# Slot attention's last group: six complete token tiles' outputs are made inside the last levels of its scan

## What is computed

```python
q, k = short_conv(h @ Wq, cq), short_conv(h @ Wk, ck)
v, w = short_conv(h @ Wv, cv), l2norm(short_conv(h @ Ww, cv))
g, beta = log_sigmoid(h @ Wf1 @ Wf2), sigmoid(h @ Wb)
# scan over the tokens, 16 heads of 128 x 128 states Sk and Sv:
#   Sk = Sk * exp(g) + k (beta w)^T ;  Sv = Sv * exp(g) + (beta w) v^T
#   o = softmax(q Sk / sqrt(128)) Sv
gate = h @ Wg1 @ Wg2 + bg2
o = o * rsqrt(mean(o * o) + EPS)
o = o * norm_w * sigmoid(gate)
x = x + o @ Wo
```

## Time and profile before

| what | us |
|---|---|
| median of 3 runs (lowest, highest) | 2630.3 (2629.23, 2631.29) |
| the profiled execution's own time | 2630.27 |
| its span in the profile | 2628.5 |
| PE busy | 2331.3 (89%) |
| DVE, ACT, POOL busy | 1678.3, 1192.8, 1100.5 |

### The profile page before, as it was taken

How to read it: one execution, slowest core, us unless ns; L and a number is a source line. 1 busy time by engine, 2 the same in 40 slices (tenths; PEclk the granted TensorE clock), 3 DMA queues, 4 the chain that set the end, 5 groups by cost and what they waited for, 6 DMA issues and landing times. The chain is left out here.

```text
span 2628.5 us, 49074 instructions
## 1 busy us (share of the span) xinstructions
PE 2331.3 (89%) x18400; PEld 1614.6 (61%) x18400; DVE 1678.3 (64%) x3286; ACT 1192.8 (45%) x2937; POOL 1100.5 (42%) x1264
## 2 busy tenths in 40 slices
PE   5888888888888889888858999999889989999999
PEld 3467754777547775477745666677533356666685
DVE  3857777577776777667726777752366557777613
ACT  3655465554554546545424555532115535555411
POOL 0367632676326763277634544430030025444300
PEclk9999999999999999999978999999889989999999
DMA  2100000000010000000004000000100030000000
GB/s 46 49 6 2 2 17 32 6 2 2 17 33 5 3 2 17 17 2 2 2 1 120 19 19 19 7 1 1 49 1 1 1 114 19 19 19 13 1 1 17
DMA packets 57625, 46.30 MB, mean 18 GB/s; under 512 B 11560, under 2 KB 50864, under 8 KB 57008
## 3 DMA queue, kind: packets, MB, share of 16 engines
q1 hardware_dynamic: 57392, 43.16, 5.6%
HBM read 42.10 MB, written 1.05 MB: 16 GB/s over the span
## 5 line engine op out<-in xcount | busy, mean ns | idle before, releaser
L1153 DVE SCALAR_TENSOR_TENSOR work<-four,taps,work 128x511 f32<-128x511 f32 (+2 forms) x384 | 284.7, 748 | 127.1 <-ACT work L849 117.5
L1761 POOL TENSOR_TENSOR rot<-q_plain,ropes 128x512 f32<-128x512 f32 x64 | 81.0, 1266 | 574.7 <-ACT q_plain L1792 574.7
L599 PE MATMUL four<-xT,wring 128*128 128x512 f32 x512 | 252.8, 621 | 6.6 <-DMA wring<-in_Wk_dram 4.8
L906 ACT ACTIVATE work<-four 128x512 f32<-128x512 f32 x216 | 129.0, 597 | 269.4 <-PE four L678 243.4
L729 PE MATMUL four<-work 128*128 128x128 f32 x1536 | 217.0, 286 | 0.0
L1805 ACT ACTIVATE pr<-four,nmaxf 128x512 f32<-128x512 f32 (+3 forms) x256 | 133.8, 525 | 171.4 <-DVE nmaxf L1643 171.4
L1643 DVE TENSOR_REDUCE nmaxf<-four 128x1 f32<-128x512 f32 (+3 forms) x256 | 125.7, 491 | 125.6 <-PE four L1486 120.8
L729 PEld LDWEIGHTS four<-work 128*128 128x128 f32 x1536 | 193.4, 196 | 3.9
L1484 PE MATMUL four<-rot,rot 128*128 128x512 f32 (+3 forms) x512 | 179.5, 446 | 5.5 <-DVE rot L1635 3.8
L1088 POOL TENSOR_TENSOR work<-work 128x256 f32<-128x256 f32 x184 | 145.6, 791 | 78.0 <-DVE work L1217 57.4
L1095 POOL TENSOR_TENSOR work<-work 128x256 f32<-128x256 f32 x184 | 141.7, 770 | 84.2 <-PE bank L763 74.6
(11 more groups left out here) (266 smaller groups left out, 5430.9 us busy)
## 6 DMA issues: line engine op xcount, KB each, us to landing
wqkv<-in_f_wq_dram SPq DMA_DIRECT2D x32, 128.0 KB, 2.3
wqkv<-in_f_wk_dram SPq DMA_DIRECT2D x32, 128.0 KB, 2.4
wqkv<-in_f_wv_dram SPq DMA_DIRECT2D x32, 128.0 KB, 2.4
wo<-in_f_wo_dram SPq DMA_DIRECT2D x2, 2048.0 KB, 11.7
we<-in_f_we_dram SPq DMA_DIRECT2D x4, 1024.0 KB
wring<-in_Wk_dram SPq DMA_DIRECT2D x4, 512.0 KB, 3.8
wring<-in_Ww_dram SPq DMA_DIRECT2D x4, 512.0 KB
wring<-in_Wv_dram SPq DMA_DIRECT2D x4, 512.0 KB, 3.9
```

The source lines that it names most:

```text
L599: last = nc.tensor.matmul(unit_bank(i)[:], wring[n % 2][:, c, h * P:(h + 1) * P], k.xT[:, c, b * T:(b + 1) * T], start=(c == 0), stop=(c = ...
L906: nc.scalar.activation(turned_keys(s, l), b3(key_bank), ACT.Copy).then_inc(key_kept, 1)
L1153: ins = nc.vector.scalar_tensor_tensor(out=cbuf[i % 4][:, n:], in0=unit_bank(i)[:, 0:T - n], scalar=taps[:, {"q": 0, "k": 1}.get(kind, 2), ...
```

## The change

The tiles of the last group are taken in a new order, 0, 1, 2, 4, 5, 6 and then 3 and 7 (`LAST_TILES`, `tile_of`). Eight steps are woven into the scan's end: `LATE` gives e = 0 to 5 to (s, j) = (8, 1) to (8, 6), e = 6 to (9, 0) and e = 7 to (9, 1). In step e, at the end of the level's own work:

- PE makes gate(e), then turn_y(e - 1) for e = 1 to 6, then result(e - 2) for e = 2 to 7;
- ACT does open_gate(e) and keep_y(e - 1);
- DVE does bias(e), scale_y(e - 1), add(e - 2);
- POOL scales tile e (for e up to 5), and at (8, 0), after its decay (6,4), takes the root of the six complete tiles (24 elements per partition).

Behind the scan POOL takes the root of the other two tiles (8 elements) and scales them, and turn_y, keep_y, result and add follow for these two. All eight gates are made in the scan. The last group's gate, y and yT buffers lie in work areas that are free by then, and its three products use PSUM banks 0, 2 and 3. The first of each waits for the last use of its bank.

```diff
+LATE = {(B * CH, j): j - 1 for j in range(1, LEVELS)} | {(B * CH + 1, 0): LEVELS - 1, (B * CH + 1, 1): LEVELS}
+LAST_TILES = [b * CH + c for b in range(B) for c in range(CH - 1)] + [b * CH + CH - 1 for b in range(B)]
+NEARLY = B * (CH - 1)
...
+        tile_banks = lambda g: (k.bank[0], k.bank[2], k.bank[3]) if g == NG else (gate_bank, y_bank, result_bank)
...
+                def last_outputs(e):
+                    gate(NG, e)
+                    if 1 <= e <= NEARLY:
+                        turn_y(NG, e - 1)
+                    if 2 <= e <= NEARLY + 1:
+                        result(NG, e - 2)
...
                     if g == NG:
-                        gate(g, 0)
-                        for t in range(NT):
-                            if t + 1 < NT:
-                                gate(g, t + 1)
-                            turn_y(g, t)
-                            if t:
-                                result(g, t - 1)
+                        turn_y(g, NT - 2)
+                        turn_y(g, NT - 1)
+                        result(g, NT - 2)
                         result(g, NT - 1)
                         break
...
+                            if late(g, s, j) is not None:
+                                last_outputs(late(g, s, j))
...
+                def last_outputs(e):
+                    open_gate(NG, e)
+                    if 1 <= e <= NEARLY:
+                        keep_y(NG, e - 1)
...
+                def root(n, squares, out, shape):
+                    p = power[:]
+                    for _ in shape[2:]:
+                        p = p.unsqueeze(2)
+                    nc.gpsimd.tensor_scalar(out, squares, 4.0 / P, 4.0 * EPS, ALU.mult, ALU.add).then_inc(o_var, 1)
+                    pool.wait_ge(o_var, n)
+                    nc.gpsimd.tensor_tensor(out, out, p.broadcast_to(shape), ALU.pow).then_inc(o_rstd, 1)
+                    pool.wait_ge(o_rstd, n)
...
+                    if g == NG:
+                        pool.wait_ge(out_squared, g * SLOTS * HG)
+                        root(g + 1, by_chunk(ss_o)[:, :, CH - 1], by_chunk(rt_o)[:, :, CH - 1], [P, B, HG])
+                        weigh(g, NT - 2)
+                        weigh(g, NT - 1)
...
+                            if g + 1 == NG and (s, j) == (B * CH, 0):
+                                pool.wait_ge(out_squared, g * SLOTS * HG + NEARLY * HG)
+                                root(NG, by_chunk(ss_o)[:, :, 0:CH - 1], by_chunk(rt_o)[:, :, 0:CH - 1], [P, B, CH - 1, HG])
+                            if late(g, s, j) is not None and late(g, s, j) < NEARLY:
+                                weigh(NG, late(g, s, j))
...
+                def last_outputs(e):
+                    bias(NG, e)
+                    if 1 <= e <= NEARLY:
+                        scale_y(NG, e - 1)
+                    if 2 <= e <= NEARLY + 1:
+                        add(NG, e - 2)
```

More of the change, by code:

```diff
@@ L473, in chunk @@
             return ap[:, b, :, c * P:(c + 1) * P]
+        last_gt = [work[:, n * 512:n * 512 + 512] for n in range(2)]
+        last_y = [work[:, n * 512:n * 512 + 512].rearrange(hv, h=HG) for n in range(2, 4)]
+        last_yT = [work[:, n * 512:n * 512 + 512].rearrange(hv, h=HG) for n in range(4, 6)]
+        gate_of = lambda g, n: (last_gt if g == NG else gt)[n % 2]
+        y_of = lambda g, n: (last_y if g == NG else y)[n % 2]
+        yT_of = lambda g, n: (last_yT if g == NG else yT)[n % 2]
+        tile_banks = lambda g: (k.bank[0], k.bank[2], k.bank[3]) if g == NG else (gate_bank, y_bank, result_bank)
         unit_bank = lambda i: k.bank[(0, 2, 3)[i % 3]]
@@ L571, in turn_y @@
[L571 to L574, removed]
+                        if g == NG:
+                            pe.wait_ge(key_kept, g * len(KEY_TURNS))
+                        else:
+                            pe.wait_ge(pair_used, g * len(PAIRS))
+                    nc.tensor.matmul(tile_banks(g)[0][:], low_g[:, t * P:(t + 1) * P], wg2[:], start=True, stop=True).then_inc(gate_made, 1)
@@ L575, in turn_y @@
+                def turn_y(g, n):
+                    pe.wait_ge(y_ready, (g - 1) * NT + n + 1)
+                    if n:
+                        pe.wait_ge(y_kept, (g - 1) * NT + n)
+                    elif g == NG:
+                        pe.wait_ge(score_used, g * len(SCORES))
                     for h in range(HG):
-                        last = nc.tensor.transpose(y_bank[:, h * P:(h + 1) * P], y[t % 2][:, h], k.eye[:])
+                        last = nc.tensor.transpose(tile_banks(g)[1][:, h * P:(h + 1) * P], y_of(g, n)[:, h], k.eye[:])
@@ L577, in turn_y, with result @@
                     last.then_inc(y_turned, 1)
[L579 to L582, removed]
+                def result(g, n):
+                    pe.wait_ge(y_kept, (g - 1) * NT + n + 1)
+                    pe.wait_ge(x_added, (g - 1) * NT + n + 1)
+                    if n == 0 and g < NG:
                         pe.wait_ge(out_copied, g * SLOTS)
@@ L892, in _ @@
                     if g == NG:
[L893 to L897, removed]
+                        keep_y(g, NT - 2)
+                        keep_y(g, NT - 1)
                         break
@@ L1130, in bias @@
                         dve.wait_ge(rest_in, g * 48)
[L1131 removed]
+                    nc.vector.tensor_tensor(gate_of(g, t), tile_banks(g)[0][:], bg2[:], ALU.add).then_inc(gate_biased, 1)
                 def scale_y(g, t):
@@ L1179, in _ @@
                     if g == NG:
-                        bias(g, 0)
-                        for t in range(NT):
-                            if t + 1 < NT:
-                                bias(g, t + 1)
-                            scale_y(g, t)
-                            if t >= 2:
-                                add(g, t - 2)
+                        scale_y(g, NT - 2)
+                        scale_y(g, NT - 1)
                         add(g, NT - 2)
```

47 lines of the change are left out of this document (26 added, 21 removed).

## The result

The changed kernel took 2625.7 us (median of 20 runs, 2621.2 to 2631.1), the kernel before 2631.0 beside it (20 runs): a ratio of 0.9978, 95% interval 0.9970 to 0.9985, 5.3 us or 0.2% faster. The forecast was 2621.6, its range 2615 to 2631. The profiled execution took 2625.92 us with a span of 2624.1.

A forecast was written before the change was run, and what follows sets the result against it. In the last 75 us no engine is full; the chain of hand-overs bounds. Output phase 31.0 us less, scan's end 22.3 later: 8.7 us off the 2630.3 median gives 2621.6, range 2615 to 2631 (own range 2618.5 to 2625).

The forecast's parts named there:

- Root of six tiles: In the scan on POOL before decay (6,5): a power of 24 elements takes 4.06 us, decay 3.8 late.
- Rival A: Power costs per instruction: 1.35 us more in the scan, 4.06 more behind it, time 2627.0; chance 0.10.
- Six scalings hidden: POOL's six scalings in the scan, 1.1 us each, are hidden in longer levels; without that cover 0.2 us each.
- First gates and y: Before slot 7's levels: first gates and first y make own_pair(7) 6.6 us late and pair(7,0) 5.7 late.
- The forecast by the Trainium skill's rule: At the scan's root: power blocks DVE's two-input instructions until 1309.4, transposes some 0.9 us later; 2622.5, not counted in the sum.
- Five levels of 5.2: Woven levels e = 2 to 6 each contain the complete 4.63 us tile loop: 5.2 us each, 26.0 for five.
- Scan's end 22.3 later: From pair(7,6) through outputs(7), keep_out and squares: POOL's root starts at 1354.7 instead of 1332.43, 22.3 us later.
- What is left: Behind the scan, two tiles without gates take 15.2 us where the output phase took 46.2: 31.0 us less.
- the sum's base: Whole kernel: change only the span and subtract from the 2630.3 us median, groups 0 to 2 running the same instructions.
- B: Clock stays at 1.2 GHz through the woven levels: about 22 us more, 2643; chance 0.08, milder form another 0.10.
- C: Clock never falls or is back before outputs(6), as in group 0: 2615 to 2618 us; chance 0.12.
- D: Woven levels lengthened by POOL and DVE in each other's way: 0.7 us more per level, 4 us, 2625.6; chance 0.08.

The follow-up runs named there:

- POOL's part alone: Against the kernel before, only the root of six tiles and their six scalings moved into the scan; 2620.5 us, ratio 0.9976.

## Why the prediction was right, and where not

To compare, I add 3.9 us to each time of the prediction, as product (6,4) started so much later.

1. *Root of six tiles.* 4.06 us expected, 4.15 measured. With 5.41 for 32 elements and 1.63 for 8, a power costs 0.37 us and 0.158 a further element. Rival A falls by these rows.
2. *Six scalings hidden.* Right: POOL is idle 3.49 us in the woven level. Without that cover they cost 0.15 us each (POOL's part alone, levels of 1.9).
3. *First gates and y.* own_pair(7) was due at 1316.4 + 3.9 = 1320.3 and came at 1319.86; pair(7,0), due at 1323.7, at 1324.16. Two errors cancelled here by luck: the start was 0.4 us early, and what follows took 4.3 us in place of 3.4, because in this trace the clock did not come back in outputs(6), as taken, but in gate(2) behind it:

```profile
1319.86:1324.16 4.30, 4.30 (x49) 4.01 (x48) 0.89 (x2) 0.69 (x1) 0.00 (x0) 0.50 0.00 0
```

In the second and third trace of the changed kernel it came back in outputs(6). The forecast by the Trainium skill's rule ("SBUF — State Buffer", "Who interferes with whom"), 2622.5 with the power holding up DVE's instructions with two SBUF inputs, did not show: L1330 took 0.42 and L1306 0.69 inside the power's 4.15 us. For POOL's products that rule of the Trainium skill agrees with the rows (DVE's scaling at 1.39, its decay at 0.92), for POOL's power it does not, and there the measurement decides.
4. *Five levels of 5.2.* Measured 5.37 on average, 26.9 us in place of 26.0. The step is right in its form: the serial loop was in every level. Its content was a little off: contention lay less in the scaling (0.79 beside 0.68) and more in DVE's decay L1330: 0.92 us where POOL's decay had started 0.03 ahead of it (1335.75), and 0.42 at 1309.63. In the first of the five (5.63) the clock, still at half at its start, has a part; the other four average 5.31. The last level was 3.16 for 3.15.
5. *Scan's end 22.3 later.* Measured 1359.89 - 3.93 - 1332.43 = 23.5: 0.4 us from step 3 and 0.9 from step 4. The step itself took 5.71 us for 5.75.
6. *What is left.* 15.2 expected, 13.46 measured. The mis-sized terms are the two results: 3.62 and 3.65 were taken, the clock came back inside the first, and they took 2.97 and 2.0 with their hand-overs. The power of 8 elements was 0.3 us longer than taken (1.63 for 1.35).

*Sum.* 32.7 - 23.5 = 9.2 against 31.0 - 22.3 = 8.7. The errors of steps 5 and 6 were about 1.2 and 1.7 us and cancelled in part, which is luck.

*The step that failed is the sum's base*: "I change the span only and subtract from 2630.3. Groups 0 to 2 run the same instructions as before." The same instructions do not take the same time. The median fell by 5.3 and not 9.0. Some 1.6 us of the difference stand behind the stretch, where the clock falls (on the mean of four traces each, 1.1 us late against 0.5 early, and the 0.5 is one trace's). The other 2 us stay open. The interval lets the 5.3 be up to 7.9, which is still under 9.0, and the same shortfall came on the second chip; no trace ties it to a place.

*Rivals.* B (levels at 1.2 GHz) did not come: the levels ran at 0.98. C, the clock back before outputs(6), came once, in the changed kernel's last trace: pair(7,0) stood 14.5 us behind (6,4), not 16.8. There the clock fell in the first woven level instead, which took 7.13 us. The stretch was 65.57, only 0.6 under the mean: what the clock gave at one place it took at the next. D had the mechanism (POOL and DVE in each other's way) at 4 us; it was 0.9 at most, with a part of that the clock's.

The forecast's own range (2618.5 to 2625) missed the median by 0.7 us, the full one held it. The measured 0.22% is just over the 0.2% that the forecast took as the border between the same and faster; the interval, 0.15 to 0.30%, does not reach zero.

## What to carry to other kernels

Work that is woven into a loop saves no more than its own serial chain allows: if gate, bias, tanh, scaling and transposes meet inside one step, the step is no shorter than the old loop (5.3 us, where the loop was 4.63). Move the consumer's input one step ahead, and only the fullest engine counts (3.6 us, PE at 100%); the test is whether the fullest engine still has idle time with a releaser in the woven step. And state a small gain by the stretch that the change touches as well as by the whole time: each of the two parts around it moved by up to 7 us between executions of the same instructions here.

## What the runs showed of the hardware

- POOL's power is priced by the element: 1.63, 4.15 and 5.41 us for 8, 24 and 32 elements in each partition, while a product of 32 elements takes 0.25.
- The power held up neither DVE instruction with two SBUF inputs that ran beside it (0.42 and 0.69 us inside its 4.15); POOL's scaling of 128x512 beside the scaling of y makes that 1.39 us in place of 0.68; POOL's decay, started just ahead, makes DVE's 0.92 in place of 0.42.
- Six products without a use kept the granted clock at 1.00 through a wait for POOL, and shortened what stood behind by 1.9 us.
- A clock that comes back earlier is not always a gain: in eight of nine traces with woven tiles PE was through with the projections sooner, went on at half clock behind its next wait and was 1.2 to 1.7 us late in the end. In one trace of the kernel before, the clock came back early, PE waited as long, the clock stayed full and 2.1 us were gained; what decides between the two is not shown.
